# Softmax exponentials split and turned by transposing DMAs, one per head, instead of TensorE transposes; contexts two heads later, expert loads in pieces

## What is computed

```python
# third block: hidden_q = layernorm(x), kv_r = rotated context, H = 16 heads, L = 256 keys, D_C = 64
q_r    = einsum('bshq,hqr->bhsr', rope(q_big), W_qr)
k_r    = einsum('bld,hdr->bhlr', kv_r, W_kr)
scores = einsum('bhsr,bhlr->bhsl', q_r, k_r)
attn   = softmax(scores, axis=-1)
ctx_c  = einsum('bhsl,bld->bhsd', attn, kv_r)
x      = x + tanh(g_xattn[1]) * (per-head projections of ctx_c, summed, @ Wo.T)
# fourth block: top 2 of 8 experts per row, 320 slots per expert
h      = relu(buf @ w1[e] + b1[e]);  out_e = h @ w2[e] + b2[e]
```

## Time and profile before

| | us |
|---|---|
| median of 3 runs | 506.84 |
| lowest and highest run | 502.27, 507.36 |
| profiled execution | 504.92 |
| its span | 503.1 |
| TensorE busy in the span | 446.0 (89%) |
| VectorE busy | 383.9 (76%) |
| ScalarE busy | 283.0 (56%) |
| GpSimd busy | 214.9 (43%) |

### The profile page before, as it was taken

The page is one execution under the profiler, slowest core; times in us unless marked ns, Lnnn a source line. Parts: engine busy times, 40 slices in busy tenths (PEclk is TensorE's granted clock), DMA queues, the critical chain, the costliest instruction groups (busy, mean ns, idle before and its releaser), DMA issues.

```text
span 503.1 us, 12039 instructions
## 1 busy us (share of the span) xinstructions
PE 446.0 (89%) x4681; PEld 341.6 (68%) x4688; DVE 383.9 (76%) x881; ACT 283.0 (56%) x626; POOL 214.9 (43%) x281
## 2 busy tenths in 40 slices
PE   3966998898899999998999899898789999999994
PEld 3435565357677777787877777676577677777773
DVE  4459999468678888897888688786658888877992
ACT  2677687674345666564566454466317455566660
POOL 3267150102323233352554365333523477787533
PEclk9997899899999999999999999999999999999998
DMA  8993005900530000000061000000103776667832
GB/s 273 265 342 61 1 1 167 382 25 1 161 135 2 1 1 3 2 1 1 1 212 45 2 1 24 24 22 9 45 2 104 237 189 160 161 177 213 206 33 26
DMA packets 37721, 46.76 MB, mean 93 GB/s; under 512 B 7584, under 2 KB 33056, under 8 KB 37472
## 3 DMA queue, kind: packets, MB, share of 16 engines
q1 hardware_dynamic: 32912, 40.82, 25.5%
q0 software_dynamic: 4224, 4.79, 6.0%
q10 hardware_dynamic: 528, 0.38, 0.3%
HBM read 40.14 MB, written 8.55 MB: 97 GB/s over the span
## 4 chain that ended last, share of the span: by engine, by line
PE 59%; DVE 20%; ACT 10%; issue 6%; POOL 2%; DMA 1%; another core or an unknown queue 1%; POOLq 0%; ACTq 0%; DVEq 0%
PE psum L2032 10%; PE psum L2045 7%; PE psum L1755 7%; PE psum L1859 3%; DVE lw L1201 3%; PE psum L1822 2%; PE psum L1815 2%; DVE lw L1261 2%; PE psum L1680 2%; PE psum L1899 2%; DVE nmax L1256 2%; DVE lw L1199 2%; PE psum L1873 2%; PE psum L1840 2%; PE psum L2054 2%
## 5 line engine op out<-in xcount | busy, mean ns | idle before, releaser
L587 POOL TENSOR_TENSOR lw<-lw 128x512 f32<-128x512 f32 x48 | 60.7, 1269 | 110.5 <-DVE lw L1201 109.2
L1755 PE MATMUL psum<-lp 128*128 128x256 f16 x576 | 69.6, 276 | 2.1 <-DVE i L1314 2.1
L895 ACT ACTIVATE lw<-psum,nmax 128x256 f32<-128x256 f32 x128 | 59.3, 469 | 21.2 <-DVE nmax L1256 21.0
L902 ACT ACTIVATE lw<-psum 128x512 f16<-128x512 f32 x64 | 38.2, 597 | 43.4 <-PE psum L1859 43.4
L1755 PEld LDWEIGHTS psum<-lp 128*128 128x128 f16 x576 | 54.7, 99 | 9.3 <-DVE i L1314 2.4
L2032 PE MATMUL psum<-lw,se 128*128 128x320 f16 x384 | 54.4, 299 | 2.0 <-DVE lw L1460 1.2
L977 ACT ACTIVATE lw<-psum,b1w 128x320 f16<-128x320 f32 x64 | 33.7, 527 | 39.8 <-PE psum L2032 39.5
L1261 DVE TENSOR_TENSOR lw<-psum,lw 128x512 f16<-128x512 f32 x64 | 43.4, 679 | 15.0 <-ACT lw L902 14.6
L685 POOL DMA_INDIRECT out_x<-lw,tslot x24 | 42.6, 1775 | 20.7 <-DVE lw L1507 11.4
L2032 PEld LDWEIGHTS psum<-lw,se 128*128 128x128 f16 x384 | 36.6, 97 | 18.0 <-DVE lw L1460 1.6
L1859 PE MATMUL psum<-identf,lw 128*128 128x128 f32 x256 | 40.8, 282 | 7.3 <-DVE lw L1261 5.1
(11 more groups left out here) (249 smaller groups left out, 1016.1 us busy)
## 6 DMA issues: line engine op xcount, KB each, us to landing
se<-in_w SPq DMA_DIRECT2D x16, 1024.0 KB
dispatch<-in_empty SPq DMA_DIRECT2D x4, 662.5 KB, 9.6
lw<-dispatch SPq DMA_DIRECT2D x8, 265.0 KB
lp<-in_Wq SPq DMA_DIRECT2D x2, 1024.0 KB, 9.7
se<-in_WoT SPq DMA_DIRECT2D x1, 2048.0 KB, 12.1
lp<-in_w_kc_q SPq DMA_DIRECT2D x2, 768.0 KB, 10.0
x_sb<-in_x SPq DMA_DIRECT2D x2, 512.0 KB, 6.5
se<-in_gate_wT SPq DMA_DIRECT2D x1, 1024.0 KB, 9.3
```

Source lines behind the costliest of these rows:

```text
L587: nc.gpsimd.tensor_tensor(rope[:, c % QT, :], t1[:, c % 2, :], t2[:, c % 2, :], ALU.add)\
L895: A_(e_sb[:, n % 2, st * S:(st + 1) * S], bank[3 + n % 2][:, st * S:(st + 1) * S], ACT.Exp, bias=nmax[:, n % 2, st:st + 1], accum_out=esum ...
L902: A_(at[0][:, n % 2, :], turn_bank(n)[:, :], ACT.Copy).then_inc(a_at, 1)
L1755: ins = M(tile_bank(c)[:, half * S:(half + 1) * S], m1[w][:, kc, half, col:col + P], (yth, ytl)[a][:, kc, b * S:(b + 1) * S], start=(n == ...
```

## The change

- The exponentials are split before they are turned: `exps_high(n)` (ScalarE) copies `e_sb` to fp16 in `hl[:, n % 2, 0:512]`, `exps_low(n)` (VectorE) writes the rest to `hl[:, n % 2, 512:1024]`. Both read SBUF, where `at_high` and `at_low` read PSUM.
- `turned_exps(n)`: SP issues one transposing DMA per head, `hl[:, n % 2, :]` (128 x 1024 fp16, 256 KB) into `turned[n % 3]`, as eight 128x128 blocks. It waits for the low half, and for the context three heads back. `turn_scores` is gone (256 TensorE transposes), and so is its PSUM bank's use; bank 5 now serves routing for all batches but the last.
- `exps_high(n)` waits for the transfer of head n - 2, since it overwrites its source.
- `context(n)` waits for its transfer and runs two loop steps after the head in place of one.
- ScalarE's loop does both high halves of a pair at even n and both exps of the next pair at odd n; VectorE's does both maxima at odd n, the low halves at even n (the second one at the end of the step), qz_low ahead of the turns, ct_low at h = 3 and norm at h = 1 in place of 2 and 0. Query tiles come one per step at h = 1, 2, 3, in place of one at h = 2 and two at h = 3.
- The weights of experts 0 and 1 come as eight DMAs of 256 KB each, one per head behind the transposing DMA (n = 0 to 7 and 34 to 41), b2 as six DMAs at n = 8 to 13; the stores of x move into the same loop. Three of the four splits come four steps later.
- After the loop the order of contexts, row selection, norm and projection changes; `turned[2]` lies in the last two tiles of `y_sb`.

The core of the diff (left out: semaphore names, the routing functions that take `route_bank(b)` for `bank[0]`, and the counts waited for):

```diff
@@ -40,7 +40,7 @@
 ENDS = (0, NE - 2, NE - 1)
 TURN = (0, 2, 1, 3)
 NHR = 6
-SPLITS = (8, 12, 16, 32)
+SPLITS = (12, 16, 20, 32)
 NWARM = 24
 def program(nc, A, out):
     ctx = ExitStack()
@@ -146,13 +146,14 @@
         qT = w1([2, D + P], BF16)
         w2 = carve(lw, 34)
-        w2([4 * 256])
+        hl = w2([2, 1024], F16)
         t1 = w2([2, 512])
         t2 = w2([2, 512])
         rope = w2([QT, 512])
         qz = [w2([2, 512], F16) for _ in range(2)]
         e_sb = w2([2, 512])
-        at = [w2([2, 512], F16) for _ in range(2)]
+        turned = [w2([1024], F16) for _ in range(2)] + [y_sb[:, NT - TPB:NT, :].rearrange("p a b -> p (a b)").bitcast(F16)]
+        turned = [a.rearrange("p (w st lt s) -> p w st lt s", w=2, st=TPB, lt=TPB) for a in turned]
         cxn = w2([512])
         ct = [w2([512], F16) for _ in range(2)]
         nmax = sb("nmax", [P, 2, TPB])
@@ -338,7 +340,7 @@
             g, h = n // G, n % G
-            return [c for c in {2: [QT * (g + 2)], 3: [QT * (g + 2) + 1, QT * (g + 2) + 2]}.get(h, []) if c < QT * NGB]
+            return [QT * (g + 2) + h - 1] if h >= 1 and g + 2 < NGB else []
         def routed(n, at):
@@ -349,9 +351,9 @@
             return bank[(0, 1, 0)[c % QT]]
-        def turn_bank(n):
-            return bank[1] if n in (NHB - 3, NHB - 1) else bank[5]
+        def route_bank(b):
+            return bank[5] if b < B - 1 else bank[0]
         def pair_of(b):
             return slice(TPB * b, TPB * b + TPB)
@@ -432,17 +434,44 @@
             sp.wait_ge(p_set, KB)
             sp.wait_ge(v_u1, NT)
             sp.wait_ge(p_ks, 2 * NG)
-            sp.dma_start(b2b, A["b2"].partition_broadcast(P)).then_inc(d_b, 16)
-            for j in range(2):
-                sp.dma_start(b2c[j * W3:(j + 1) * W3], A["b2"][:, j * P:(j + 1) * P].partition_broadcast(W3)).then_inc(d_b, 16)
+            def output_bias(j):
+                if j < 4:
+                    es = slice(2 * j, 2 * j + 2)
+                    sp.dma_start(b2b[:, es, :], A["b2"][es, :].partition_broadcast(P)).then_inc(d_b, 16)
+                else:
+                    j -= 4
+                    sp.dma_start(b2c[j * W3:(j + 1) * W3], A["b2"][:, j * P:(j + 1) * P].partition_broadcast(W3))\
+                        .then_inc(d_b, 16)
             def weights(e):
-                if e >= 1:
+                sp.wait_ge(v_we, 4 * e)
+                sp.dma_start(eraw[:, 0, :].rearrange("p (a b) -> p a b", a=KC),
+                             A["w1"][e].rearrange("(a p) n -> p a n", p=P)).then_inc(d_e, 64)
+                sp.dma_start(eraw[:, 1, :].rearrange("p (a b) -> p a b", a=MH),
+                             A["w2"][e].rearrange("(a p) n -> p a n", p=P)).then_inc(d_e, 64)
+            def weight_part(e, j):
+                if e >= 1 and j == 0:
                     sp.wait_ge(v_we, 4 * e)
-                sp.dma_start(eraw[:, 0, :].rearrange("p (a b) -> p a b", a=KC),
-                             A["w1"][e].rearrange("(a p) n -> p a n", p=P)).then_inc(d_e, 16)
-                sp.dma_start(eraw[:, 1, :].rearrange("p (a b) -> p a b", a=MH),
-                             A["w2"][e].rearrange("(a p) n -> p a n", p=P)).then_inc(d_e, 16)
+                a, half = j // 2, slice(j % 2 * EH // 2, (j % 2 + 1) * EH // 2)
+                if j < 4:
+                    sp.dma_start(eraw[:, 0, a * EH:(a + 1) * EH][:, half], A["w1"][e, a * P:(a + 1) * P, half])\
+                        .then_inc(d_e, 16)
+                else:
+                    a = 2 * (j - 4)
+                    sp.dma_start(eraw[:, 1, a * D:(a + 2) * D].rearrange("p (a b) -> p a b", a=2),
+                                 A["w2"][e, a * P:(a + 2) * P, :].rearrange("(a p) n -> p a n", p=P)).then_inc(d_e, 16)
+            def turned_exps(n):
+                sp.wait_ge(v_at, n + 1)
+                if n >= 3:
+                    sp.wait_ge(p_cx, n - 2)
+                sp.dma_start_transpose(turned[n % 3].rearrange("p w st lt s -> p (w st lt) s"), hl[:, n % 2, :])\
+                    .then_inc(d_at[n % 2], 16)
             def dispatched(e):
                 if e == 0:
@@ -456,18 +485,27 @@
                 sp.dma_start(slots_u[W3:2 * W3, e % 2, 2, D:D + 1 + NE], buf_d[e * CAP + 2 * P:(e + 1) * CAP, D:D + 1 + NE])\
                     .then_inc(d_slot[e % 2], 16)
-            weights(0)
-            weights(1)
-            for b in range(B):
-                if b == B - 1:
+            def rows_out(b):
+                sp.wait_ge(v_u2, b + 1)
+                sp.dma_start(out_v[:, pair_of(b), :], x_sb[:, pair_of(b), :]).then_inc(d_out, 16)
+            for n in range(NHB):
+                turned_exps(n)
+                if n < 8:
+                    weight_part(0, n)
+                elif n < 14:
+                    output_bias(n - 8)
+                elif 34 <= n < 42:
+                    weight_part(1, n - 34)
+                for b in routed(n, 6):
+                    rows_out(b)
+                if n == NHB - 2:
                     sp.wait_ge(p_qz, NGB)
                     sp.dma_start(iotac, A["iotac"]).then_inc(d_sel, 16)
-                sp.wait_ge(v_u2, b + 1)
-                if b == B - 1:
-                    dispatched(0)
-                    dispatched(1)
-                sp.dma_start(out_v[:, pair_of(b), :], x_sb[:, pair_of(b), :]).then_inc(d_out, 16)
+            dispatched(0)
+            dispatched(1)
+            rows_out(B - 1)
             for e in range(NE):
                 if e + 2 < NE:
                     dispatched(e + 2)
@@ -888,18 +926,18 @@
                 g, h = n // G, n % G
                 act.wait_ge(v_max, n + 1)
                 if n >= 2:
-                    act.wait_ge(p_at, n - 1)
+                    act.wait_ge(v_at, n - 1)
                 if h == 0 and g >= 2:
                     act.wait_ge(v_norm, g - 1)
                 for st in range(TPB):
                     A_(e_sb[:, n % 2, st * S:(st + 1) * S], bank[3 + n % 2][:, st * S:(st + 1) * S], ACT.Exp,
                        bias=nmax[:, n % 2, st:st + 1], accum_out=esum[:, g % 2, st, TURN[h]:TURN[h] + 1]).then_inc(a_exp, 1)
-            def at_high(n):
-                act.wait_ge(p_at, n + 1)
+            def exps_high(n):
+                act.wait_ge(a_exp, TPB * (n + 1))
                 if n >= 2:
-                    act.wait_ge(p_cx, n - 1)
-                A_(at[0][:, n % 2, :], turn_bank(n)[:, :], ACT.Copy).then_inc(a_at, 1)
+                    act.wait_ge(d_at[n % 2], 16 * (n // 2))
+                A_(hl[:, n % 2, 0:512], e_sb[:, n % 2, :], ACT.Copy).then_inc(a_at, 1)
             def ct_high(g):
                 act.wait_ge(p_ct, g + 1)
@@ -910,7 +948,7 @@
             def split_high(k):
                 e, q = k // 4, k % 4
-                act.wait_ge(d_e, 32 * (e + 1))
+                act.wait_ge(d_e, 128 * (e + 1))
                 if e >= 2:
                     act.wait_ge(p_oe, 3 * (e - 1))
                 A_(we[q // 2][0][:, e % 2, (q % 2) * EH:(q % 2 + 1) * EH],
...
@@ -934,15 +972,17 @@
             qz_high(0)
             exps(0)
             yth_of(B - 1)
+            exps(1)
             for n in range(NHB):
                 g, h = n // G, n % G
                 for b in routed(n, 12):
                     route_exp(b)
                 if n % 2 == 0:
+                    exps_high(n)
+                    exps_high(n + 1)
+                elif n + 1 < NHB:
                     exps(n + 1)
-                at_high(n)
-                if n % 2 == 1 and n + 1 < NHB:
-                    exps(n + 1)
+                    exps(n + 2)
                 if h == 1 and g + 1 < NGB:
                     qz_high(g + 1)
                 if h == 2 and g >= 1:
@@ -1256,9 +1296,10 @@
                 V.tensor_reduce(nmax[:, n % 2, :], bank[3 + n % 2][:, :].rearrange("p (a b) -> p a b", a=TPB),
                                 AX.X, ALU.max, negate=True).then_inc(v_max, 1)
-            def at_low(n):
+            def exps_low(n):
                 dve.wait_ge(a_at, n + 1)
-                V.tensor_tensor(at[1][:, n % 2, :], turn_bank(n)[:, :], at[0][:, n % 2, :], ALU.subtract).then_inc(v_at, 1)
+                V.tensor_tensor(hl[:, n % 2, 512:1024], e_sb[:, n % 2, :], hl[:, n % 2, 0:512], ALU.subtract)\
+                    .then_inc(v_at, 1)
             def norm_sums(g):
                 dve.wait_ge(a_exp, TPB * G * (g + 1))
...
@@ -1398,21 +1439,23 @@
             turn(5)
             for n in range(NHB):
                 g, h = n // G, n % G
-                if n % 2 == 1 and n + 1 < NHB:
+                if n % 2 == 0:
+                    exps_low(n)
+                elif n + 1 < NHB:
                     maxima(n + 1)
+                    maxima(n + 2)
                 if h == 0 and g >= 1:
                     norm_sums(g - 1)
-                at_low(n)
-                if h == 0 and g >= 1:
-                    norm(g - 1)
-                if n % 2 == 1 and n + 2 < NHB:
-                    maxima(n + 2)
```

(55 more changed lines are left out.)

32 lines of the change are left out of this document (16 added, 16 removed).

## The result

The changed kernel takes 531.56 us (median of 4 runs, 528.85 to 534.38) against 505.84 us of the kernel before, measured beside it (502.27 to 507.36): ratio 1.054, 95% interval 1.048 to 1.060. It is 26 us slower; the forecast was 511 us.

A forecast was written before the change was run, and what follows sets the result against it. The prediction took VectorE's program and waits to bound the attention loop. It added +3.4 us (loop) and +2.4 (end) to the profiled 504.92, giving 510.7, taken as 511 us; own range 504 to 516, whole range 488 to 542.

The forecast's parts named there:

- The sign: Whole kernel: slower was given 0.46, same 0.32 and faster 0.22.
- TensorE's turns go: Attention loop: 256 fp32 transposes leave, TensorE's queue gets 28 to 41 us shorter, and VectorE is what remains.
- exps_low at no cost: VectorE's low half in the loop: 0.60 us between starts with both inputs in SBUF, no change.
- VectorE's waits in the new order: Loop: VectorE waits 2.0 us a group for qz_high; a plain group takes 12.65 us against 12.34, +0.3.
- the +3.4 of the sum: Loop: 11 groups at 0.31 us more each, as three of 14 groups with turns already wait 2.03 us.
- Landing: Transposing DMA per head: lands in 3.0 us, costs nothing up to 3.2; each us above costs 16 us in all.
- The pieces: Weight loads of 256 KB beside the transfers in the loop: up to 3 us, taken as 0 because of slack.
- The end: Behind the last exp: high halves, low half and transfer take 4.8 us in place of 2.4, +2.4.
- the faster case: Rival, 24%: in the loop waits for L902 go and exps_low gets 0.1 us cheaper, giving 487 us.
- landing of 3.2 to 5 us: Rival, 24%: late transfers in the loop hold up ScalarE, then VectorE; 525 us at 4.0, 542 at 5.0.
- The rate: Rival, 9%: transfers take longer than a head (3.2 us), so 64 transfers set the loop: 545 to 580 us.
- TensorE's relief: Rival, 24%: relief reaches VectorE in the loop if its qz wait stays under 1.7 us a group; 487 us.

The follow-up runs named there:

- context_twice: The changed kernel with every context computed twice, which gives TensorE back its work: ratio 1.070 to the kernel before.
- low_psum_hl4: The changed kernel with four source buffers for the transfers and one PSUM input in 43 of 64 low halves: ratio 1.018 to the kernel before.
- hl4: The changed kernel with four buffers in place of two for hl, the source of the transfers: ratio 1.045 to the kernel before.
- weights_whole: The changed kernel with b2 and the experts' weights again loaded whole instead of in pieces: ratio 1.055 to the kernel before.
- no_transfer: The changed kernel with four buffers for hl and no transposing DMA, context reading hl itself: ratio 1.039 to the kernel before.
- before_low_sbuf: The kernel before, with only the low half's first input moved from PSUM to SBUF (e_sb): 510.85 us against 501.29, ratio 1.020.
- rotate_one_input: The changed kernel with GpSimd's rotation reading one tensor in place of two: ratio 1.031 to the kernel before.
- low_psum: The changed kernel with 43 of 64 low halves taking one input from PSUM: median 525.96 us, ratio 1.038 to the kernel before.
- low_pool_hl4: The changed kernel with four buffers for hl and the low half on GpSimd in place of VectorE: ratio 1.060 to the kernel before.

## Why the prediction was right or wrong

The sign was forecast as the likeliest of the three, and the time lies in the range of 488 to 542, but most of the 26 us comes from a cause that the prediction does not contain, and the range was made that wide for another one. The hit is luck. By its own steps:

1. **TensorE's turns go: right in kind.** Its busy time in the loop fell by 18.9 us, not by 28 to 41. The loop's clock is 0.96 against 0.99, and at the lower level (1.2 GHz) its instructions are longer: twelve products of L1928 took 2.74 us in the stretch behind the loop where the clock was 0.51, and 1.48 at full clock. How much of the missing relief that explains no run separates. That VectorE sets the period and not TensorE was right: context_twice gave TensorE its work back for 1.8 us of loop.
2. **exps_low at no cost: wrong, and the main error.** The prediction bounded the instruction between 0.5 and 0.69 us, the upper bound from L1487, whose two inputs lie in SBUF and which has 320 columns. 0.68 is right when it runs alone. What no bound covered was a second engine: with it the mean is 952 ns, 17.4 us more of VectorE's time, and the rotation has 7.3 us more of GpSimd's. The Trainium skill (SBUF — State Buffer, SBUF: two separate sides) states this very rule: a VectorE instruction with two SBUF inputs and a GpSimd instruction that reads SBUF take a shared pair of ports, whichever starts first keeps it for the whole instruction, and the other blocks. The prediction left it out. The traces agree with it: the second ends 0.54 or 0.55 us behind the rotation's end on VectorE, 1.12 us behind on GpSimd, and with an input in PSUM nothing gets longer.
3. **VectorE's waits in the new order: right.** 2.0 us a group for qz_high was forecast and 29.2 / 15 = 1.95 measured. In the changed kernel the blocking hides the sum, but low_psum_hl4 shows it, whose first 16 heads all have an input in PSUM and no late transfer. Its first full group without a split or routing work (timeline, start of qz_low at n = 5 and n = 9) takes 174.31 - 161.65 = 12.66 us, where the prediction had 12.65:

```profile
161.65 0.69 DVE L1292 TENSOR_TENSOR lw<-psum,lw 128x512 f16<-128x512 f32 x1 [1.89 <-ACT lw L925]
...
174.31 0.69 DVE L1292 TENSOR_TENSOR lw<-psum,lw 128x512 f16<-128x512 f32 x1 [1.89 <-ACT lw L925]
```

Groups with the same extra work in both kernels take 13.90 us against 13.61 before, and 13.22 against 12.95. So the 0.3 us a group did come, and the loop of 213.3 us against 210.4 is not far from the +3.4 of the sum. (The 12.34 us of before are a group without a ct_low yet, but the 12.95, a full one with one update, says the same.)

4. **Landing: 3.0 us forecast, medians of 3.2 and 3.3 measured** (hl4), right at the point of 3.2 that the prediction named; in low_psum_hl4 the medians by buffer are 3.1 to 3.8. The trace's 65,536 records of 256 B have a mean of 24 ns, not the 62 of the upper bound, and the 1024 of one transfer are moved in 1.4 us when nothing else runs. Of the two estimates from the Trainium skill weighed there (VectorE: DVE Perf Modes, The three transpose paths, whose 1309 ns are for one block in bf16; DMA: Bandwidth & Descriptors, Latency and other measured facts), eight blocks one after another in 10.5 us do not hold here, and 1.0 us for the data is near, but a third short.
5. **The pieces: wrong.** This term was taken as 0, with up to 3 us at most; the loop with late transfers is 5.0 us longer than with four buffers and 4.8 longer than without the pieces. The argument was that they meet only transfers with slack; exps_high waited 13 times, 14.0 us, and 9.6 us of that went with the pieces (weights_whole).
6. **The end: +2.4 forecast, 3.2 measured, the cause not shown.** From the start of the last low half to the first expert product it was 376.7 - 358.55 = 18.15 us and is 399.7 - 378.40 = 21.3. The whole stretch behind the last low half grew by 4.1. But the last transfer, to which the prediction put it down, is not shown to be the reason: without any transfer (no_transfer) that stretch is 148.8 us, against 144.5 before and 148.6 after. TensorE's clock is lower just there (windows view, the first 5 us or so behind the last low half, before and after, columns as above), and it is busy 2.0 us longer up to the first expert product; no run separates that either.

```profile
359.00:364.00 5.00, 3.51 (x38) 2.69 (x37) 2.48 (x8) 0.60 (x1) 2.12 (x3) 1.00 0.24 85
```

```profile
378.00:383.00 5.00, 3.77 (x35) 2.87 (x33) 2.44 (x7) 0.85 (x2) 3.83 (x4) 0.51 0.89 173
```

The range was to start at the faster case's time, which is 487 by its own sum and not 488; nothing hangs on it. The rivals: landing of 3.2 to 5 us would have given 525 to 542, and the time fell there, but four buffers alone give back only some 5 of the 26 us. The rate does not bind: with no transfers at all the loop is as long (228.1 us against 227.5 in hl4). TensorE's relief did not reach VectorE, as there is a wait of 1.95 us for qz where that rival needed less than 1.7.

Of the 26 us, then: the exclusion and the late transfers beside pieces together 18 (low_psum_hl4). How they share it depends on which goes first: the exclusion 8 with two buffers and 13 to 14 with four, the late transfers 5 with the exclusion whole and 10 without most of it. In the 8 or 9 us left lie the low halves that still had two SBUF inputs, the 0.3 us a group and the end of 3 to 4 us; each is seen in the traces, but no run takes them apart.

## What to carry to other kernels

When an operand moves from PSUM to SBUF, count the SBUF inputs of the instruction that reads it and look at what GpSimd does at the same moment: a VectorE instruction that goes from one SBUF input to two takes turns with GpSimd, and the price is the blocked time, not the instruction's own. A duration read where nothing was in its way is a lower bound, so bound a new instruction also by its neighbours on other engines. A wait can be filled only with work that nobody downstream is waiting behind, and loads cut in pieces are not free once a tight transfer goes out between them.

## What the runs showed of the hardware

- VectorE (two SBUF inputs) and GpSimd take strict turns, instruction by instruction, in every meeting of the traces of the changed kernel, before_low_sbuf and rotate_one_input: the second ends 0.55 us (VectorE, 512 columns) or 1.12 us (GpSimd, two inputs), 0.47 (GpSimd, one input) after the first has ended. One PSUM input on VectorE removes it wholly (low_psum, 0.64 to 0.69 us throughout).
- A transposing DMA of 128 x 1024 fp16, SBUF to SBUF, lands 3.2 to 3.3 us after its issue in hl4 (medians; 3.1 to 3.8 in low_psum_hl4), of which the data take 1.4; SP's own instruction takes 1.23 us, against 0.58 for a plain piece of 256 KB.
- GpSimd's subtraction of 512 columns to fp16 took 1.16 us (median, low_pool_hl4), its fp32 addition 1.27, its one-input form 0.62.
- Putting TensorE's busy time in the loop back from 177.7 to 196.9 us (context_twice) left the granted clock at 0.96.
